# A column list, maxima by scans and three sums per group in the attention passes of a graph network

## The reference

```
h = x @ Wn + bn
for l in range(4):
    Q, K, V = h @ WQ[l], h @ WK[l], h @ WV[l]
    scores = sum(Q[dst] * K[src], -1) * scale
    seg_max = segment_max(scores, dst)
    e = exp(scores - seg_max[dst])
    messages = segment_sum(e / segment_sum(e, dst)[dst] * V[src], dst)
    h = layernorm(h + messages @ WO[l])
```

## Time and profile before

| | |
|---|---|
| median of 3 runs (lowest to highest) | 10363.44 us (10360.34 to 10364.31) |
| the profiled execution: device time | 10346.03 us |
| its span, first to last instruction | 10344.4 us |
| TensorE, matmul | 3424.3 us busy (33%) |
| VectorE | 4701.0 us busy (45%) |
| ScalarE | 2355.7 us busy (23%) |
| GpSimd | 6863.7 us busy (66%) |

### The profile page before, as it was taken

How to read it: one execution, slowest core, us unless ns; L and a number is a source line. 1 busy time by engine, 2 the same in 40 slices (tenths; PEclk the granted TensorE clock), 3 DMA queues, 4 the chain that set the end, 5 groups by cost and what they waited for, 6 DMA issues and landing times. The chain is left out here.

```text
span 10344.4 us, 91366 instructions
## 1 busy us (share of the span) xinstructions
PE 3424.3 (33%) x16460; PEld 2885.9 (28%) x16461; DVE 4701.0 (45%) x14342; ACT 2355.7 (23%) x7156; POOL 6863.7 (66%) x7106
## 2 busy tenths in 40 slices
PE   4122213233332234232243224444443232242223
PEld 3011102222332223222232224233332222232223
DVE  6544433555545554555545555688885111121111
ACT  0000002222322223222232223244443122210000
POOL 1377775777677775777667773566664677737775
PEclk8555555666666666666666666766665566666666
DMA  1100001121111221112211121333331311111111
GB/s 33 35 2 2 2 9 36 54 54 54 44 51 54 54 54 41 54 54 54 47 48 54 54 54 26 99 89 90 89 89 42 80 53 53 53 43 53 53 53 52
DMA packets 347232, 519.21 MB, mean 50 GB/s; under 512 B 209706, under 2 KB 226628, under 8 KB 346992
## 3 DMA queue, kind: packets, MB, share of 16 engines
q0 software_dynamic: 242720, 480.17, 17.4%
q1 hardware_dynamic: 98518, 35.44, 1.5%
q10 hardware_dynamic: 5882, 2.34, 0.1%
HBM read 468.15 MB, written 49.31 MB: 50 GB/s over the span
## 5 line engine op out<-in xcount | busy, mean ns | idle before, releaser
L1166 POOL DMA_INDIRECT rows<-table_d,meta x3328 | 3177.7, 955 | 1113.1 <-issue 1006.9
L1186 PE MATMUL ps_total<-weighted_rows,ident 128*128 128x129 f32 (+1 forms) x8320 | 1780.3, 396 | 3763.4 <-ACT weighted_rows L1205 1561.4
L1186 PEld LDWEIGHTS ps_total<-weighted_rows,ident 128*128 128x128 f32 x8320 | 1606.5, 277 | 3937.5 <-ACT weighted_rows L1205 3069.4
L1271 DVE TENSOR_TENSOR prod<-rows,q_rows 128x258 f32<-128x258 f32 x1664 | 627.4, 425 | 1384.4 <-DMA rows<-table_d,meta 865.9
L1166 POOL DMA_INDIRECT rows<-pairs_d,meta x832 | 809.1, 972 | 451.2 <-issue 239.2
L1205 ACT ACTIVATE weighted_rows<-rows,corr 128x129 f32<-128x129 f32 x3328 | 998.8, 389 | 6.7
L966 POOL DMA_INDIRECT list_out_d<-tile_rec,tile_idx x784 | 813.9, 1038 | 254.3 <-issue 246.2
L1026 POOL DMA_INDIRECT tile_rows<-table_d,tile_meta x833 | 786.3, 944 | 264.4 <-issue 253.2
L1026 POOL DMA_INDIRECT tile_rows<-rows_d,tile_meta x833 | 785.8, 943 | 264.4 <-issue 253.6
L1035 DVE TENSOR_TENSOR sums<-sums,tile_sums 128x129 f32<-128x129 f32 x98 | 28.4, 290 | 1823.2 <-PE tile_sums L1076 1823.2
L1232 DVE SCALAR_TENSOR_TENSOR sums<-sums,corr,ps_total 128x129 f32 x1696 | 594.5, 351 | 412.3 <-DVE sums L1232 180.6
(11 more groups left out here) (489 smaller groups left out, 5477.2 us busy)
## 6 DMA issues: line engine op xcount, KB each, us to landing
rows<-table_d,meta POOLq DMA_INDIRECT x3328, 2.5
tile_rows<-table_d,tile_meta POOLq DMA_INDIRECT x833, 2.5
tile_rows<-rows_d,tile_meta POOLq DMA_INDIRECT x833, 2.5
rows<-pairs_d,meta POOLq DMA_INDIRECT x832, 2.8
list_out_d<-tile_rec,tile_idx POOLq DMA_INDIRECT x784, 2.1
meta<-list_in_d SPq DMA_DIRECT2D x260, 32.0 KB
tiles<-tiles_in_d SPq DMA_DIRECT2D x260, 0.0 KB
table_d<-h_rows,perm_in POOLq DMA_INDIRECT x245
```

What stands on the lines that cost most here:

```text
L1166: pool.indirect_dma_start(rows[q][:, j, 0:width], None, table_d, bass.IndirectOffsetOnAxis(meta[q][:, j, number:number + 1], 0)).then_inc( ...
L1186: mm = pe.matmul(total[:, b, 0:W], k.ident[:], wide[:, j % WS, :], start=(j == b * J), stop=(j == b * J + J - 1))
L1271: own(dve.tensor_tensor(prod[:, js, :], rows[q][:, js, :], k.q[:, ds(tk[b], 1), :].to_broadcast([P, J, P + 1]), ALU.mult))
```

## The change

The list's unit becomes one column. A tile gets exactly as many columns as its largest in-degree, but at least 8 (`LEAST`), so a group of 16 spans at most three tiles, which follow each other. A group's two words hold its first tile and, for each column, in two bits, how many tiles further it is; and a row of 16 marks (`resets_d`) tells where a tile begins.

- `order_nodes` maps 1024 columns to a row instead of 512 blocks, makes the map twice (which tile a column is in, and whether it is the first of its tile), packs the words and stores two arrays instead of one.
- SyncE loads three things for a group; the third goes to all 128 partitions.
- In attention a column's score is one instruction, a product that accumulates its sum. In the heads layer products are per column too, and one reduction follows.
- Negated scores are laid out in a row with the value that came from the group before ahead of them. A scan forward takes the running minimum of each tile, and a scan backward gives every column its tile's whole minimum. Maxima are no longer kept per node: the last value of the row is carried to the next group.
- TensorE clears three sums of a group with bf16 zeros and adds each column to one of the three at a register address; PSUM holds two groups' sums. It reads the words itself.
- VectorE adds a group's sums to `acc` with one corrected sum for the first tile and one copy for the two others.
- In the heads layer GpSimd waits for the weighting in halves of 8 columns, and VectorE weights in two halves.
- `fetch_layer` moves from the small block into the pass.

```diff
-J_IN = 2
-BLOCKS = 16 // J_IN
+LEAST = 8
+PAIRS = S // 2
...
-                own(dve.tensor_scalar(nb_i[:], most[:], float(J - 1), None, ALU.add))
-                own.wait()
-                own(dve.tensor_scalar(nb_i[:], nb_i[:], int(np.log2(J)), None, ALU.arith_shift_right))
...
+                own(dve.tensor_scalar(nb[:], most[:], float(LEAST), None, ALU.max))
...
-                            sp.dma_start(tiles[q][:], tiles_d[ds(g, 1), :]).then_inc(listed[q], 16)
+                            sp.dma_start(words[q][:], words_d[ds(g, 1), :]).then_inc(listed[q], 16)
+                            sp.dma_start(resets[q][:, 1:S + 1], resets_d[ds(g, 1), :].rearrange("a s -> (a s)").partition_broadcast(P)
+                                         ).then_inc(listed[q], 16)
...  tensor engine
-                                for j in range(b * J, b * J + J):
-                                    mm = pe.matmul(total[:, b, 0:W], k.ident[:], wide[:, j % WS, :], start=(j == b * J),
-                                                   stop=(j == b * J + J - 1))
+                            clear(q)
+                            for j in range(S):
...
+                                part = pe.snap(within(step_of(loaded, j), 2))
+                                mm = pe.matmul(total[:, q, ds(part, 1), 0:W].rearrange("p a w -> p (a w)"), k.ident[:], wide[:, j % WS, :],
+                                               start=False, stop=True, skip_group_check=True)
...  vector engine, sums
-                        for b in range(B):
-                            a = k.acc[:, ds(tk[b], 1), 0:W].rearrange("p a w -> p (a w)")
-                            if mode == "attend":
-                                own(dve.scalar_tensor_tensor(a, a, corr[q][:, S + b, :], total[:, b, 0:W], ALU.mult, ALU.add))
+                        if mode == "attend":
+                            own(dve.scalar_tensor_tensor(first, first, power[q][:, :, 0], total[:, q, 0, 0:W], ALU.mult, ALU.add))
+                            own(dve.tensor_copy(k.acc[:, ds(tile + 1, 2), 0:W], total[:, q, 1:3, 0:W]))
...  vector engine, scores
-                                    own(dve.tensor_tensor(prod[:, js, :], rows[q][:, js, :],
-                                                          k.q[:, ds(tk[b], 1), :].to_broadcast([P, J, P + 1]), ALU.mult))
+                                asked = k.q[:, ds(within(tile + step_of(loaded, j), T - 1), 1), 0:w].rearrange("p a w -> p (a w)")
+                                    own(dve.scalar_tensor_tensor(prod[:, j, :], rows[q][:, j, :], -1.0, asked, ALU.mult, ALU.mult,
+                                                                 accum_out=score[:, j, :]))
...  vector engine, maxima
-                            for b in range(B):
-                                running = k.nm[:, ds(tk[b], 1), 0:R].rearrange("p a r -> p (a r)")
-                                own(dve.tensor_copy(nmo[:, b, :], running))
-                                own(dve.tensor_tensor(running, running, nmb[:, b, :], ALU.min))
-                                own.wait()
+                            own(dve.tensor_tensor_scan(flat[1], marks, flat[0], 0.0, ALU.max, ALU.min))
+                            own.wait()
+                            own(dve.tensor_tensor_scan(flat[1][:, RS - 2::-1], marks[:, RS - 1:0:-1], flat[1][:, RS - 2::-1], 0.0, ALU.max, ALU.min))
+                            own.wait()
+                            own(dve.tensor_copy(neg[1 - q][:, :, 0], upto[:, :, S]))
```

More of the change, by code:

```diff
@@ L262, with order_nodes @@
 LEVELS = 40
[L263 to L269, removed]
+WORDS = 1024
+MAPP = NG * S // WORDS
+HALF = float(2.0 ** 98)
+def order_nodes(nc, k, fill, empty, pieces_d, deg, place, words_d, resets_d, sched, perm, deg_p, runs):
     with ExitStack() as s:
@@ L1118, in edge_pass @@
[L1118 to L1121, removed]
-        corr = [buf(nc, s, f"corr{q}", [P, S + B, R]) for q in range(2)]
-        late_tiles = buf(nc, s, "late_tiles", [1, B // PACK], I32)
-        kept = buf(nc, s, "kept", [P, W]) if mode == "heads" else None
-        nothing = kept[:] if mode == "heads" else buf(nc, s, "nothing", [P, W])[:]
@@ L1126, in edge_pass @@
-        total = psum(nc, s, "ps_total", [P, B, PSW], F32)
-        WG = 1 if mode == "heads" else B
-        PER = {"attend": 4 * B + 6, "heads": 5 * B + 12}[mode]
-        epochs = nc.values_load(sched[0:1, NEP:NEP + 1], min_val=1, max_val=NEP)
+        score = buf(nc, s, "neg_score", [P, S, 1 if mode == "attend" else 8])
+        RS = R * (S + 2)
+        neg = [buf(nc, s, f"neg{q}", [P, R, S + 2]) for q in range(2)]
+        upto = buf(nc, s, "neg_upto", [P, R, S + 2])
+        breaks = buf(nc, s, "breaks", [P, R, S + 2]) if mode == "heads" else None
@@ new lines, in edge_pass @@
+        expo = [buf(nc, s, f"expo{q}", [P, R, S + 2]) for q in range(2)] if mode == "attend" else neg
+        power = [buf(nc, s, f"power{q}", [P, R, S + 1]) for q in range(2)]
+        late_word = buf(nc, s, "late_word", [1, 1], I32)
+        nothing = buf(nc, s, "nothing", [P, W], BF16)
+        total = psum(nc, s, "ps_total", [P, 2, 3, 512], F32)
+        WG = 2 if mode == "heads" else B
+        PER = {"attend": S + 8, "heads": S + 14}[mode]
+        epochs = nc.values_load(sched[0:1, NEP:NEP + 1], min_val=1, max_val=NEP)
@@ L1130, in edge_pass, with within, step_of @@
+        def within(value, most):
+            return nc.s_assert_within(value, 0, most, skip_runtime_bounds_check_because=
+                                      "the words are made on the chip from tiles under T, at most two steps in a group")
+        def step_of(loaded, j):
+            return (loaded[j // PAIRS] >> ((6 if j < PAIRS else 0) + 2 * (j % PAIRS))) & 3
         with nc.Block() as block:
@@ L1134, in _ @@
                     dve.memset(k.acc[:, :, 0:W], 0.0)
-                    dve.memset(k.nm[:], HALF)
+                    for r in range(2):
+                        dve.memset(relation[:, r:r + 1], float(1 - r))
                 if mode == "attend":
@@ L1175, in _ @@
-                    mm.then_inc(m["block_summed" if mode == "heads" else "summed"], 1)
+                    clear(0)
+                    clear(1).then_inc(m[ends], 1)
                     with pe.Fori(0, pairs) as i:
                         for q in range(2):
+                            pe.wait_ge(listed[q], i * 48 + 48)
+                            pe.sem_inc(m["pe_passed"], 1)
+                            loaded = [pe.value_load(words[q][0:1, w:w + 1], min_val=0, max_val=64 * 4 ** PAIRS - 1) for w in range(2)]
+                            pe.sem_inc(read[q], 1)
@@ L1254, in _, with first_tile @@
+                    def first_tile(word):
+                        return dve.snap(within(word & 63, T))
+                    dve.nop().then_inc(read[0], 2)
+                    dve.nop().then_inc(read[1], 2)
+                    dve.memset(nothing[:], 0.0).then_inc(m["scored"], 1)
+                    dve.memset(power[1][:, :, 0:1], 1.0)
+                    dve.memset(late_word[:], T)
                     dve.drain()
+                    dve.sem_inc(m["sum_taken"], 1)
                     dve.sem_inc(m["summed"], 1)
@@ L1276, in _ @@
-                            ex = expo[q][:, 0:S, :]
+                                    own(dve.scalar_tensor_tensor(prod[:, j, :], rows[q][:, j, :], -1.0, asked, ALU.mult, ALU.mult,
+                                                                 accum_out=score[:, j, :]))
+                                else:
+                                    own(dve.tensor_tensor(prod[:, j, :], rows[q][:, j, 0:w], asked, ALU.mult))
+                            if mode == "heads":
+                                own.wait(S)
+                                own(dve.tensor_scalar(masks[:], of_relation[q][:], -1.0, -BIG, ALU.add, ALU.mult))
@@ new lines, in _ @@
+                            marks = resets[q][:] if mode == "attend" else breaks[:].rearrange("p r s -> p (r s)")
+                            own(dve.tensor_tensor_scan(flat[1], marks, flat[0], 0.0, ALU.max, ALU.min))
+                            own.wait()
+                            own(dve.tensor_tensor_scan(flat[1][:, RS - 2::-1], marks[:, RS - 1:0:-1], flat[1][:, RS - 2::-1], 0.0, ALU.max, ALU.min))
+                            own.wait()
+                            own(dve.tensor_copy(neg[1 - q][:, :, 0], upto[:, :, S]))
```

282 lines of the change are left out of this document (145 added, 137 removed).

## The result

The changed kernel takes 9921.74 us (median of 4 runs, 9917.59 to 9925.87) against 10363.88 us of the kernel before: ratio 0.9571, 95% interval 0.9560 to 0.9583. The profiled execution took 9917.59 us, its span 9915.5, 428.9 us less than before's 10344.4.

What follows compares the result with a forecast made beforehand. GpSimd's gather issue bounds attention, VectorE's chain the heads pass. 147.6 + 53.6 + 202.2 + 21.8 + 8 - 3 = 430 us off 10346.0 gives 9916; median 17.4 above, 9933 us; 8-in-10 range 9870 to 10050.

Steps and rivals of the forecast that it cites:

- The list: In-degrees unrounded sum to 799 columns, so 25 pairs instead of 26: 800 gathers in each pass instead of 832.
- Attention, middle: First to last gather of attention passes: 800 gathers, 0.004 us added to each, 1012 us; 147.6 us less for four.
- Attention, ends: From a pass's last product to the next stage: 10.2 us instead of 23.6; 53.6 us less for four passes.
- Heads, middle: Heads pass's gathers: VectorE's 17 us a group falls under GpSimd's 20.4; 800 gathers at 1.29 us, 1032 us, 202.2 less.
- rival 2: VectorE still sets the heads pass's pace, 22 us a group instead of 20.6; time 10010 us; chance 17%.
- 0.016 for more company of VectorE: Heads pass: 0.016 us added to each gather's 0.970 + 0.304 us, giving 1.29 us.
- Heads, end: From the heads pass's last gather to its end: 28 us instead of 49.8; 21.8 less.
- Starts and list: Starts of the four attention passes gain 8 us through moved loads; making the list loses 3 us.
- The rule against the change: Skill page: VectorE instructions with two SBUF inputs contend with GpSimd's SBUF reads, the later fully blocked; trace agreed only weakly.
- rival 1: Each gather waits out VectorE's two-operand instruction: attention +860 us, heads +365; time 11160 us, slower; chance 5%.
- Only bursts do: Argument against blocked gathers: single products lie beside gathers without lengthening them; only bursts lengthen them.
- Rivals 3 to 5: Pairs stay 26: 10136 us, 3%; attention contention or late list: 10015, 10%; VectorE or TensorE outgrows attention group: 10300 up, 3%.

## Why the prediction was right

The mechanism was right: the gathers' number and GpSimd's pace set every pass, and VectorE drops out of the heads pass. That the profiled execution took 9917.6 us for 9916 is luck: the middle of attention gave 43.4 us more than forecast and its ends 3.3, the middle of heads 33.0 less, starts and list 5.6 less, and 9.6 were lost that the sum didn't have. The median, 9921.7 for 9933, is lower because I added the 17.4 us between before's profiled execution and its median; after's lie 4 apart.

- *The list:* right, 25 pairs; the pair undone alone gives 205 us of windows back.
- *Attention, middle:* 191.0 us for 147.6. The step "I add 0.004 us to each, because VectorE reads two SBUF operands for longer" had the wrong sign: not busy time counts, but how much of an instruction is left when a gather begins inside it. Before, 0.011 us of the 1.2607 came from two-column products; 1.2500 instead of my 1.2650 a gather makes 48 us, of which 5 go off because before's other three windows were shorter than the first.
- *Attention, ends:* 56.9 us for 53.6, partly by luck. In the first pass the stretch that I forecast, from the last product on, takes 12.2 us and not 10.2 (whose items add up to 10.05): TensorE took 6.79 us, within the 6 to 9 expected, but ended 3.0 us after ScalarE and not 0.8. Made up for is this by a piece that the sum didn't have: the last product ends 3.6 us after the last gather instead of 5.8.
- *Heads, middle:* 169.2 for 202.2. That VectorE drops out as the bound was right, so rival 2 fell. Mis-sized was "0.016 for more company of VectorE": it measured 1027 - 970 = 57 ns a gather. Long two-operand instructions now fall beside gathers, while before GpSimd stood waiting during the weighting and so met it once in the whole pass. The taken-away wait came back in part as contention.
- *Heads, end:* 27.9 us for 28.
- *Starts and list:* 5 us of gain expected, 0.6 of loss measured. The list's making costs 4.2 us (3 expected): the same memset between it and the first pass (L1752, before L1714) starts at 1712.8 instead of 1708.6. Counted from there the first pass starts 3.0 us sooner than before, so its first gather comes 1.2 later; from the stage after a pass to the next gather it is 0.7, 1.6 and 3.4 us less, but 5.1 more ahead of the heads pass, which no run explains.
- *Not in the sum:* 9.6 us after the heads pass, mainly the clock in the last stage.

*The rule against the change.* The hold of rival 1 is real, at another price: a gather that begins inside a two-operand instruction waits for its end (0.81 us more in the weighting, 0.37 in a scan), then isn't held by the next long one, and an operand in PSUM removes the wait. The Trainium skill ("SBUF — State Buffer", section "Who interferes with whom") says that a VectorE instruction with two SBUF inputs contends with GpSimd's reads, that in contention the later one is fully blocked, and that with one SBUF input, outside the two-port modes, there is none; the trace agrees, from the weighting (1.76 us) down to single products (0.94 to 1.05). The page also infers that such an instruction doesn't hold up the writing of descriptors. No run here separates that from the gather's reading of its row numbers in `meta`, and the gather of 0.96 us, which lay beside the second half once under way, does not speak against the inference.

Two readings of mine were wrong. "Only bursts do", of what lengthens a gather: in before's first pass one that began 0.07 us into a product of two columns that stands alone took 1.17. And "no row here shows a full block": the trace of before had one, the gather of 2.90 us above. Rival 1's time still didn't come, since it made every product cost 0.27 us; only the few gathers begun inside one pay, and in the attention passes after the change that is less than 1 us a pass. The hold counts where a gather meets long instructions: 50 x 1.32 = 66 us in the heads pass. Rivals 3 to 5 didn't come.

## To carry to other kernels

Where GpSimd's gathers pace a pass, first count them, then look for gathers longer than the rest and read which VectorE instruction they begin inside: how much of it is left and whether both operands are in SBUF decide, not VectorE's share of busy time. A single such gather in the trace of before is worth a look, since the change may bring one in every group. Putting one operand in PSUM frees the gathers even if it costs VectorE a copy more, as long as VectorE has slack; here that gave 35 us more, from one comparison to another (ratio 0.9530 for 0.9571). An engine relieved from waiting meets work it never met before, so price the contention at the new overlap, not the old.

## What I had not expected of the hardware

- A gather begun inside a VectorE instruction with two SBUF operands ends at a fixed time after that instruction, 0.82 us for products and weighting, whether 0.42 or 2.29 us long, 0.75 for a scan of 287 values and 0.71 for the masks' addition. Why these differ is open.
- Short VectorE products that start every 0.20 us held one gather for 3.2 us, while eight pieces of 256 elements that start every 0.34 us held it for 0.1 to 0.2 in most cases. In the records both overlap by 0.08 us. Why the one leaves an opening and the other doesn't is open.
